# Feed-forward layernorms folded into weights and factors; the special tokens' chain in slots of the steps

## The reference, cut to what matters

```python
x = x + attn_a(_layernorm(x))      # linear attention, 16 heads: q, k = elu + 1; out @ Wo + bo
x = x + ffn(_layernorm(x))         # sq_relu(xf @ Ws1) @ Ws2, and routed experts times trunc(prob)
x = x + attn_b(_layernorm(x))      # only the first 16 tokens of each sequence attend
x = x + ffn(_layernorm(x))         # the same weights
```

## Time and profile before

| what | us |
|---|---|
| median of 3 runs (lowest, highest) | 489.46 (489.21, 490.68) |
| the profiled execution's own time | 489.17 |
| its span, first to last instruction | 487.4 |
| granted PE clock, mean over the span | 0.973 |

### The profile page before, as it was taken

The page is one execution under the profiler, slowest core; times in us unless marked ns, Lnnn a source line. Parts: engine busy times, 40 slices in busy tenths (PEclk is TensorE's granted clock), DMA queues, the critical chain, the costliest instruction groups (busy, mean ns, idle before and its releaser), DMA issues.

```text
span 487.4 us, 8128 instructions
## 1 busy us (share of the span) xinstructions
PE 451.1 (93%) x2695; PEld 366.4 (75%) x2695; DVE 307.2 (63%) x788; ACT 249.3 (51%) x415; POOL 175.3 (36%) x253
## 2 busy tenths in 40 slices
PE   8899899999999997869999999999999999996763
PEld 4699788989989886758778687686878786884441
DVE  5554846564465436356687867886977977694462
ACT  3445545545545412455657455466665574756230
POOL 2354333453333501143344415452342634224300
PEclk9999999999999999879999999999999999999895
DMA  8421111121000020000211011001100110111110
GB/s 275 137 87 44 44 44 43 51 80 43 0 0 1 2 87 1 1 2 1 63 48 50 2 44 46 18 27 45 44 22 25 46 46 2 45 44 45 45 44 7
DMA packets 22659, 20.74 MB, mean 43 GB/s; under 512 B 2950, under 2 KB 22604, under 8 KB 22604
## 3 DMA queue, kind: packets, MB, share of 16 engines
q1 hardware_dynamic: 22044, 19.53, 12.8%
q10 hardware_dynamic: 560, 0.52, 0.3%
HBM read 11.53 MB, written 8.45 MB: 41 GB/s over the span
## 4 chain that ended last, share of the span: by engine, by line
PE 69%; DVE 14%; ACT 6%; POOL 5%; issue 4%; DMA 1%; POOLq 0%; DVEq 0%; ACTq 0%
PE PG L1154 11%; PE PA L1239 8%; PE PG L1244 5%; PE PA L1258 4%; DVE ln_bn L669 3%; PE PB L1244 3%; PE PT L1231 3%; ACT scratch L511 3%; PE PA L1144 3%; PE PA L1145 3%; PE PA L1146 3%; PE PB L1131 3%; PE PB L1132 3%; PE PB L1130 3%; POOL ln_rstd L429 2%
## 5 line engine op out<-in xcount | busy, mean ns | idle before, releaser
L511 ACT ACTIVATE scratch<-x_all,ln_shift,ln_rstd 128x256 f32<-128x256 f32 (+2 forms) x188 | 97.4, 589 | 74.3 <-POOL ln_shift L433 43.9
L427 POOL TENSOR_SCALAR ln_rstd<-ln_mv 128x4 f32<-128x4 f32 x48 | 10.8, 226 | 216.5 <-DVE ln_mv L672 212.8
L669 DVE BATCH_NORM_STATS2 ln_bn<-x_all 128x6 f32<-128x256 f32 (+1 forms) x188 | 65.8, 412 | 0.5
L1239 PE MATMUL PA<-scratch,ws 128*128 128x512 f32 x128 | 62.8, 614 | 1.5 <-ACT scratch L614 1.2
L1154 PE MATMUL PG<-scratch 128*128 128x256 f32 x256 | 58.0, 379 | 1.3 <-DVE scratch L749 1.3
L749 DVE SCALAR_TENSOR_TENSOR scratch<-scratch,PB 128x1024 f32<-128x1024 f32 x16 | 19.5, 1221 | 60.3 <-ACT scratch L546 60.3
L1154 PEld LDWEIGHTS PG<-scratch 128*128 128x128 f32 x256 | 47.4, 190 | 7.4 <-issue 1.5
L440 POOL TENSOR_TENSOR x_all<-x_all,ob_rows 128x1024 f32<-128x1024 f32 x16 | 37.8, 2365 | 41.9 <-ACT scratch L511 41.9
L429 POOL TENSOR_TENSOR ln_rstd<-ln_rstd,minus_half 128x4 f32<-128x4 f32 x48 | 49.8, 1038 | 4.0
L1231 PE MATMUL PT<-ident,scratch 128*128 128x128 f32 x256 | 35.0, 281 | 9.9 <-ACT scratch L511 9.2
L1231 PEld LDWEIGHTS PT<-ident,scratch 128*128 128x128 f32 x256 | 28.5, 144 | 15.3 <-ACT scratch L511 11.6
(11 more groups left out here) (213 smaller groups left out, 939.1 us busy)
## 6 DMA issues: line engine op xcount, KB each, us to landing
out_dram<-scratch SPq DMA_DIRECT2D x16, 512.0 KB, 2.9
x_all<-n_L_attn_a_inputs_q_dram SPq DMA_DIRECT2D x15, 512.0 KB, 3.6
x_all<-n_L_attn_a_inputs_q_dram ACTq DMA_DIRECT2D x2, 128.0 KB, 3.1
x_all<-n_L_attn_a_inputs_q_dram SPq DMA_DIRECT2D x2, 128.0 KB, 2.9
scratch<-in_L_attn_a_Wk_dram SPq DMA_DIRECT2D x1, 256.0 KB, 4.1
scratch<-in_L_attn_a_Wq_dram ACTq DMA_DIRECT2D x1, 256.0 KB, 4.4
scratch<-in_L_attn_a_Wv_dram SPq DMA_DIRECT2D x1, 256.0 KB, 6.4
scratch<-in_L_attn_a_Wo_dram SPq DMA_DIRECT2D x1, 256.0 KB, 5.9
```

Source lines behind the costliest of these rows:

```text
L511: nc.scalar.activation(dst[:, t:t + 1, 0:width], x_tile(n, t)[:, :, 0:width], ACT.Identity, scale=ln_rstd[:, slot, t:t + 1], bias=ln_shift ...
L669: nc.vector.bn_stats(ln_bn[:, slot, t:t + 1, :], x_tile(n, t)).then_inc(bn, 1)
L1239: last = mm(dst, ws1[:, c, :], xt[:, c, :], start=(c == 0), stop=(c == C - 1))
```

## The change

Pass 1 stays. In pass 2:

1. **No normalisation of y2 and y3.** PE transposes the raw x of r. The mean goes out with the weights: `w1c` is `Ws1` less its column means. The relu is taken of twice the unscaled hidden product and squared; the FFN is homogeneous of degree two, so 1/(var + eps) is a factor on the squares. POOL's `rsq` makes it (of 4 var + 4 eps, to the power -1) from the bn_stats records; bn_aggr goes. For the first FFN the factor is turned to columns by four PE transposes of a broadcast and multiplied on (`h2s`, DVE); for the second it is applied to the result, two tiles by DVE, two by ACT (`y3`) and an add of POOL.
2. **The second hidden product from the first.** PT still holds `w1c` times x; the second FFN's is that plus `wc` times `h2s` (`wc` = Ws2 times w1c, made once) plus a bias `w1ob` from ob. PE adds one 512-column product to PT instead of two on new transposes.
3. **Shorter pipeline.** The second `down` is of two steps back, so steps run to 17; x is stored from `x_all`, and no `x_out` is needed. The o product goes to PB and PT, the Wo product and the results of the second `down` to PA. PG is left to the special tokens.
4. **The chain in slots.** `chain(i, slot)`, slots 0 to 3 of a step, replaces `prepare`, `iterate` and the code behind the last step. Weights of attn_b are folded with the 16x16 blocks and the layernorm weights, logits are 64 x 256 with queries of one sequence at a time against masked keys, the factor of q's layernorm is applied to the logits.
5. `run_experts` stands once per step in each engine, now POOL too, with both FFNs' code under one `If`. Some setup semaphores are merged.

The diff, cut to its core (a line of "..." marks what is left out):

```diff
@@ gpsimd
+            def rsq(slot, j, bn, powed, done):
+                a, d, both = ln_a[:, slot, :], ln_d[:, slot, :], ln_bn[:, slot, :, :]
+                pool.wait_ge(bn, T * (j + 1))
+                nc.gpsimd.tensor_tensor(a, both[:, :, 2], both[:, :, 5], ALU.add).then_inc(powed, 1)
+                nc.gpsimd.tensor_tensor(d, both[:, :, 1], both[:, :, 4], ALU.subtract).then_inc(powed, 1)
...
+                nc.gpsimd.tensor_tensor(ln_rsq[:, slot, :], a, minus_ones[:, :], ALU.pow).then_inc(done, 1)
...
                 if runs(r):
+                    ge(pool, r2_mm, r)
+                    rsq(0, r, bn2, pow2, rsq2)
+                if runs(v):
...
+                    rsq(1, v, bn3, pow3, rsq3)
+                if runs(r):
+                    pool.wait_ge(t2_mm, C * (r + 1))
                     add_row(nr, ob_rows, ob_added)
+                chain(i, 1)
+                if runs(v):
+                    pool.wait_ge(f4_scaled, 2 * (v + 1))
+                    last = x_all[:, nv * T + 2:(nv + 1) * T, :]
+                    nc.gpsimd.tensor_tensor(last, last, y3, ALU.add).then_inc(out_pool, 1)
@@ scalar, chain
+                elif (i, slot) == (2, 3):
+                    act.wait_ge(c_brow, 1)
+                    act.wait_ge(o_mm, 4)
+                    nc.scalar.activation(bias_all, PG[0:SP, 1, :], ACT.Copy).then_inc(c_brow_sb, 1)
+                elif (i, slot) == (3, 1):
+                    nc.scalar.activation(bias_k, PG[0:SP, 0, 3 * P:4 * P], ACT.Copy).then_inc(c_brow_sb, 1)
@@ scalar, step
-                    normalise(y3, nu, 1, u, rstd3, norm3)
+                    act.wait_ge(f4_mm, v + 1)
+                    act.wait_ge(rsq3, v + 1)
+                    ge(act, out_pool, v)
+                    for t in range(2, T):
+                        nc.scalar.activation(y3[:, t - 2:t - 1, :], four(PA)[:, t:t + 1, :], ACT.Copy,
+                                             scale=ln_rsq[:, 1, t:t + 1]).then_inc(f4_scaled, 1)
@@ vector, step
+                    dve.wait_ge(rsq3, v + 1)
+                    if v < B:
+                        dve.wait_ge(c_xs, 16 * (v + 1))
+                    for t in range(2):
+                        nc.vector.scalar_tensor_tensor(x_tile(nv, t), four(PA)[:, t:t + 1, :], ln_rsq[:, 1, t:t + 1], x_tile(nv, t),
+                                                       ALU.mult, ALU.add).then_inc(out_dve, 1)
+                chain(i, 1)
...
+                    nc.vector.tensor_tensor(h2s, h2, PT[:, 1, :], ALU.mult).then_inc(f1_scaled, 1)
+                chain(i, 2)
...
+                if at in SOFTMAX:
+                    it = SOFTMAX[at]
+                    dve.wait_ge(c_logit, it + 1)
+                    dve.wait_ge(c_rs, it + 2)
+                    link(nc.vector.tensor_tensor(heads(lg), heads(PG[0:SP, 0, 0:D]), over_feats(inv_std[it + 1]), ALU.mult))
+                    link(nc.vector.reduce_max(mx16, heads(lg), AX))
+                    nc.vector.tensor_tensor(heads(lg), heads(lg), over_feats(mx16), ALU.subtract).then_inc(c_lg, 1)
@@ tensor, step
+                if runs(r):
+                    pe.wait_ge(w_added, r + 1)
+                    for c in range(C):
+                        for t in range(T):
+                            last = nc.tensor.transpose(PA[:, c, t * P:(t + 1) * P], x_all[:, nr * T + t, c * P:(c + 1) * P], ident[:, :])
+                        last.then_inc(t2_mm, 1)
                 if runs(i):
...
+                    for k in (6, 7, 0, 1, 2, 3, 4, 5):
                         t, c = k // C, k % C
+                        if k == 0:
+                            ge(pe, f2_added, i - 1)
...
                 if runs(v):
                     pe.wait_ge(f3_sq, v + 1)
+                    pe.wait_ge(t2_done, min(C * (r + 1), C * NG))
+                    down(PA, h3, f4_mm)
+                chain(i, 1)
                 if runs(r):
...
+                        last = mm(PT[:, 0, :], w1c[:, c, :], x2t[:, c, :], start=(c == 0), stop=(c == C - 1))
+                    last.then_inc(f1_mm, 1)
...
                 if runs(r):
+                    pe.wait_ge(rsq2, r + 1)
+                    for t in range(T):
+                        last = nc.tensor.transpose(PT[:, 1, t * P:(t + 1) * P], ln_rsq[:, 0, t:t + 1].to_broadcast([P, P]), ident[:, :])
+                    last.then_inc(r2_mm, 1)
+                chain(i, 2)
...
-                    transposes(PT, y3, t3_mm)
                 if runs(r):
+                    pe.wait_ge(f1_scaled, r + 1)
+                    mm(PT[:, 0, :], wc, h2s, start=False, stop=True, skip_group_check=True).then_inc(f3_mm, 1)
+                chain(i, 3)
+                if runs(r):
+                    down(PB, h2s, f2_mm)
+                    run_experts(r, nr, i)
@@ tensor, chain
+            T_LIN = {(6, 2): 0, (10, 2): 1, (12, 2): 2}
+            LOGITS = {(8, 2): 0, (10, 3): 1, (12, 3): 2}
+            T_PROB = {(8, 3): 0, (11, 1): 1, (13, 1): 2}
+            VALUES = {(9, 1): 0, (11, 2): 1, (13, 2): 2}
+            T_OUT = {(9, 2): 0, (11, 3): 1}
+            NEXT_Q = {(9, 3): 1, (12, 1): 2}
...
+                elif at == (3, 1):
+                    pe.wait_ge(c_wts, 16 * 4)
+                    pe.wait_ge(c_brow_sb, 2)
+                    for w in range(2):
+                        for c in range(C):
+                            for o in range(C):
+                                last = mm(PG[:, w, c * D + o * P:c * D + (o + 1) * P], raw4[w][:, o, c * P:(c + 1) * P], l_bd[w], start=True, stop=True)
+                    last.then_inc(c_fold, 1)
...
+                elif at == (6, 1):
+                    pe.wait_ge(c_zt_sb, 1)
+                    for dst, cols in ((PG[0:SP, 0, :], slice(0, 2 * D)), (PG[0:SP, 1, 0:D], slice(2 * D, 3 * D))):
+                        for c in range(C):
+                            last = mm(dst, zz_t[:, c, :], w_qkv[:, c, cols], start=(c == 0), stop=(c == C - 1))
+                    last.then_inc(c_qkv, 1)
...
+                if at in LOGITS:
...
+                    for c in range(C):
+                        for b in range(B):
+                            last = mm(PG[0:SP, 0, c * P:(c + 1) * P], q_one[:, c, b * SP:(b + 1) * SP], kn_mask[:, c, b, :],
+                                      start=(b == 0), stop=(b == B - 1))
+                    last.then_inc(c_logit, 1)
```

More of the change, by code:

```diff
@@ L268, in four @@
             return pair[:, :, :].rearrange("p b (t d) -> p (b t) d", d=D)
-        def turned_o(i):
-            return PT if isinstance(i, int) and i == 0 else PG
         def x_group(n):
@@ L365, in _ @@
                 sp.dma_start(dst, rows(w)).then_inc(c_wts, 16)
-            for b in range(B):
-                step(0, b)
-            sp.wait_ge(o_mm, B)
-            for dst, v in ((ob_b, ob), (lna_b, lna_w), (lnb_b, lnb_w)):
-                sp.dma_start(dst, row(v).to_broadcast([SP, D])).then_inc(c_vecs, 16)
-            for dst, w in zip(l_rows, (lqw, lkw, lvw)):
-                for h in range(HC):
-                    sp.dma_start(dst[h * HD:(h + 1) * HD, :], w).then_inc(c_vecs, 16)
-            with nc.allow_non_contiguous_dma(reason="two short bias vectors, features on partitions"):
-                for dst, v in ((qb_col, qb), (vb_col, vb)):
+            sp.wait_ge(o_mm, 1)
@@ L500, in _ @@
+                chain(i, 2)
+                if runs(r):
+                    run_experts(r)
+            for g in range(G):
                 for b in range(B):
                     step(g, b)
-            chain_rstd(2)
+            for b in range(2):
+                step(G, b)
         @block.scalar
@@ L609, in step @@
+                    nc.scalar.activation(h2, PT[:, 0, :], ACT.Relu, scale=2.0).then_inc(f1_relu, 1)
                     act.wait_ge(f1_relu, r + 1)
                     nc.scalar.activation(h2, h2, ACT.Square).then_inc(f1_sq, 1)
-                if runs(u):
-                    act.wait_ge(t3_mm, C * (u + 1))
-                    ge(act, f3_mm, u)
-                    nc.scalar.activation(x3t, PT[:, :, :], ACT.Copy).then_inc(t3_done, 1)
-                it = iteration(g)
-                softmax_here = it is not None and b == (1 if g == G else 2)
@@ new lines, in experts @@
+            def experts(k, p, tiles, xt, y, h):
+                for t in range(tiles):
+                    for c in range(C):
+                        last = mm(PT[0:p, 1, t * NE:(t + 1) * NE], xt[:, c, t * P:t * P + p], wr[:, c, :],
+                                  start=(c == 0), stop=(c == C - 1))
+                last.then_inc(r_logits, 1)
+                with pe.Fori(0, NE) as e:
+                    pe.wait_ge(r_w, 32 * (k * NE + e + 1))
+                    for c in range(C):
+                        last = mm(PA[:, 0, 0:tiles * p], w1e[:, c, :], xt[:, c, :], start=(c == 0), stop=(c == C - 1))
+                    last.then_inc(r_hid, 1)
+                    pe.wait_ge(r_sq, k * NE + e + 1)
+                    for t in range(tiles):
```

(3 more changed lines are left out.)

1124 lines of the change are left out of this document (576 added, 548 removed).

## The result

The changed kernel takes **457.24 us** (median of 4 runs, 457.06 to 458.77) against 489.33 (4 runs, 486.43 to 490.68) on the same chip: 0.9359 of the time before, 95% interval 0.9312 to 0.9405. The forecast was 452, its range 443 to 468. The profiled run took 457.29 us, 1.8 over its span of 455.5. A later control, the changed kernel unaltered, gave 456.98 us, ratio 0.9362 (0.9326 to 0.9397). The time lies inside the range and 0.24 us outside the narrower bounds of 447 to 457.

A forecast was written before the change was run, and what follows sets the result against it. TensorE, busy 93% of a 487.4 us span, was taken as the bound. Last write-back 422.9 (192.5 + 11.9 + 218.5), end 25.2 and clock 1.7 gave span 449.8; with 1.77 over the span, 451.6, written as 452 us, range 443 to 468.

The forecast's parts named there:

- first write-back: Step 0 of the second pass: added fold transposes and products move its start from 189.73 to about 192.5 us.
- step 1: Second pass, between the first two write-backs: no result two steps back, no `wc` or down product; 11.9 us.
- The bare step: Steady second-pass step without special-token work: 13.0 us of PE work plus waits, taken as 13.75 us against 14.94.
- The end: From the last write-back's start to the end of the span: 25.2 us, against 52.7 before.
- The clock: Early second pass: one fall to half speed kept, 1.7 us, where falls had lost 5.1 us before.
- The chain in its slots: Special-token work in steps 2 to 15, PE items priced by columns, small VectorE operations mostly fitting in gaps: 218.5 us.
- step 3's stalls: ScalarE's late bias copies hold the second down product 2.05 us and the fold products 1.45; step 21.0 us.
- Steps 11 and 13: Softmax on VectorE delays statistics, o normalisation and factor, 0.6 us each; value products find no hole; 17.2 us each.
- Rival one: GpSimd's two factors come late, with scaling and `o_hi` behind them: 14 steps, +13, 465 us; chance 0.20.
- Rival two: Fewer waits than walked: step 3's stalls partly vanish, no clock fall, 256-wide operations at low ends; 446 us; chance 0.10.
- Rival three: PE's jump over skipped expert code waits for instructions, 2.9 us in each of 16 steps: 498 us; chance 0.05.
- Rival four: Clock falls repeatedly, in steps 1 to 3 and the drain, four times 1.7 us: 458 us; chance 0.05.

## Why the prediction was right, and where it missed

The direction, the mechanism and the largest terms held; the miss is 457.24 - 452 = 5.2 us, 1.1%. On the spans: 455.5 against 449.8, +5.7 us, by terms: first write-back +0.3, step 1 -0.2, steps 2 to 15 **+7.5**, end -0.15, clock -1.7.

- **The bare step** (13.75 forecast) is 13.80, seen by itself in the kernel without a chain. The list of removed and added items in 128-column units was complete; the wait for `o_hi` is 0.36 in the records for 0.45.
- **The end** (25.2) is 25.05: the walk through waits named each releaser, and GpSimd's two factors took 2.4 to 2.5 us each, as assumed. But the sentence that explained the 52.7 us of before by the attention's third iteration and the special feed-forward was wrong for three quarters: without them the old end is still 39.7. The walk didn't lean on that sentence.
- **Step 1** is within 0.2. The **first write-back** is within 0.3, which is partly luck: it moved by 2 us between two executions of this kernel.
- **The clock:** one fall was kept at 1.7 us, and none came while TensorE was the bound. That was luck too: the control's profiled execution had one, in pass 1. Without these 1.7 us the miss would have been 6.9.
- **The step that failed is "The chain in its slots"**, in its sizes. It forecast 218.5 for steps 2 to 15 and 226.0 came. Three things made it so.
  - Step 2, +1.5: the block operations were priced as short VectorE work that fits beside the result's scaling; they stand still beside GpSimd's two adds, and moving them gave back 1.9. Holds in steps 5, 10 and 13 add 0.4, 0.14 and 0.12.
  - Chain items were priced by columns alone, while an item with a half tile (64*128 or 128*64) costs about 0.10 more on each side. Steps 2 to 15 of the changed kernel hold 24 such items. Fifteen stand outside slot 2, and at each the item ahead lasts 0.09 longer by starts (0.95 for 0.86, 1.82 for 1.73) and the one behind 0.10 longer (1.83 for 1.73). Nine stand in slot 2, ahead of the Wo product; there five small ones vanish in the wait for `o_hi`, and what the others cost behind them can't be told from that wait.
  - The items themselves last longer than priced: the small transposes 0.26 for 0.20, logits and values 1.89 for 1.74, the next q 0.58 for 0.44 (twice, and once with 0.20 of products that had no price), the bias products 2.11 for 1.96, q, k and v 2.72 for 2.6, step 7's products 1.92 for 1.72.

  An estimate from these: 15 x 0.19 = 2.85 for the sides, about 1.8 for the items outside slot 2 and 0.2 for those in it, 1.5 and 0.66 for the holds, 0.7 for 0.05 in each bare step, -0.1 for step 3's stalls: 7.6, for the 7.5 that came. The 0.10 on each side is shown by an experiment for two transposes; for the other items it is read from starts in the changed kernel.
- **Steps 11 and 13** hide a slip of the working. It names a stall of 0.6 and a lost hole in each, and its own terms for step 11 (13.75, 1.74 twice, 0.2 and 0.6) come to 18.0, but the list has 17.2. There is no such stall, and the value products still found their hole, costing 1.45 for 1.74. Measured are 17.82 and 17.93.
- **Rival one** (GpSimd's factor late, 465): no. No wait of PE in 192 to 430 us is for the factor; GpSimd does cost time, but by holding VectorE, which no rival had. **Rival two** (446): one of its conditions came (no fall of the clock), but step 3 kept its stalls. **Rival three** (jumps, 498): no; with the jumps gone the time is the same. The rule of the Trainium skill named there ("Runtime: NRT & Kernel Launch", "Instruction fetch mechanics") shows no cost in this kernel's 16 jumps; whether they leave the two fetched pages no run shows. **Rival four** (458) has the measured time, by chance: clock 1.00 in both early windows.
- Of the **signs of being right**, the write-backs of bare steps, the wait for `o_hi`, step 3 (21.34) and the last store 21.7 us behind the last write-back came; the last write-back near 423 did not (430.45), by the step named above.

The hold of VectorE could have been read ahead. In the kernel before the block operations stood where no add ran (0.69 for three), but in its first pass, where a 128x512 operation with two SBUF operands takes 0.69 (at 58.72), a like one had lasted 2.40, until 0.55 behind the end of GpSimd's add. From its timelines of VectorE and GpSimd:

```profile
55.68 2.40 DVE L712 TENSOR_TENSOR scratch<-scratch 128x512 f32<-128x512 f32 x1
...
58.72 0.69 DVE L783 TENSOR_TENSOR wo_lo<-scratch,wo_hi 128x512 fp32r<-128x512 f32 x1
...
55.13 2.40 POOL L440 TENSOR_TENSOR x_all<-x_all,scratch 128x1024 f32 x1
```

## What to carry to other kernels

A TensorE-bound step can be priced from columns, here to 0.05 us, but an extra item in it by its tile size and its neighbours too. Items of one tile size are best put together; that wasn't run here. Before placing small VectorE work, look at which of it reads two operands from SBUF, columns of factors included, while a GpSimd add runs. Where a change has two parts, run both kernels without one of them: here the other brought all of the gain (-34.4 us) and the new placing of the chain saved nothing, which no ratio of the whole would have shown.

## What was not expected of the hardware

- A VectorE operation of 128x128 with two SBUF operands, 0.28 us alone, lasts 1.35 to 2.43 beside a GpSimd add, to 0.15 us behind that add's end. A 64x256 operation with one tensor and two columns, all in SBUF, is held too (0.40 alone, up to 2.58); those with an operand in PSUM are not.
- A TensorE item with a 64*128 tile between full ones costs 0.10 us on each side, and by the starts so does one of 128*64; two 64-row transposes cost 0.46 us of a step, two full ones 0.23.
- A wait of 2.48 us in step 2 was followed by a granted clock of 0.60 over 3 us; waits of 1.56 and 1.80 us in the changed kernel were followed by no fall (1.00 from 207 to 222 and from 222 to 237).
